# A four-layer attention and expert kernel on one core: the orders of its stages rewritten in four tables

## What is computed

```python
# L0
x = x + gate_a * (attend(q, k, v of modulate(ln(x)), 16 heads) @ W_proj)        # 256 keys
x = x + attend(ln(x) @ W_qc, ln(ctx) @ W_kvc) @ W_cproj                          # 1601 keys
x = x + gate_m * (gelu(modulate(ln(x)) @ W_mlp1) @ W_mlp2)
# L1
nx = layer_norm(x); w = softmax((nx @ Wq) @ (ctx @ Wk).T * H ** -0.5)            # one head, 1601 keys
combined = concat([nx, w @ (ctx @ Wv), anchor])
router = softmax(combined @ router_W + router_b)                                 # 3 experts
h = silu(combined @ e_w1 + e_b1); routed = sum(router * (h @ e_w2 + e_b2))
g = sigmoid(silu(combined @ gate_w1 + gate_b1) @ gate_w2 + gate_b2)
x = x + g * (routed @ out_w + out_b)
# L2
x = x + attend(ada_ln(x, t) @ Wq, ada_ln(ctx, t) @ Wkv) @ Wp                     # 1601 keys, 16 heads
# L3
x = x + g_sa * (attend(qkv of modulate(ln(x))) @ sa_proj_w)                      # 256 keys
x = x + attend(ln(x) @ q_w, ctx @ kv_w) @ ca_proj_w                              # 1601 keys
x = x + g_ff * (gelu(modulate(ln(x)) @ fc1_w) @ fc2_w)
```

## Time and profile before

| | before |
|---|---|
| median of 3 executions | 5056.57 us (5051.58 to 5058.7) |
| the profiled execution | 5052.83 us, of which the span of the profile is 5051.0 us |
| TensorE busy | 4586.7 us, 91% of the span, 47748 matmuls |
| DVE, ACT, POOL busy | 4001.8 us (79%), 3560.8 us (70%), 1628.4 us (32%) |
| granted clock of TensorE, mean of the span | 0.975 |
| DMA | 284.41 MB, mean 56 GB/s |

### The profile page before, as it was taken

How to read it: one execution, slowest core, us unless ns; L and a number is a source line. 1 busy time by engine, 2 the same in 40 slices (tenths; PEclk the granted TensorE clock), 3 DMA queues, 4 the chain that set the end, 5 groups by cost and what they waited for, 6 DMA issues and landing times.

```text
span 5051.0 us, 122456 instructions
## 1 busy us (share of the span) xinstructions
PE 4586.7 (91%) x47748; PEld 2149.7 (43%) x47748; DVE 4001.8 (79%) x8750; ACT 3560.8 (70%) x4867; POOL 1628.4 (32%) x2319
## 2 busy tenths in 40 slices
PE   5799999999998788868999999999999999999997
PEld 2344444444443577753333343443434443333333
DVE  5799899899886444427888888888998888888885
ACT  2387788787877344434777878878787777777776
POOL 4344444444431011032333242433223232323321
PEclk9799999999999899987999999999999999999998
DMA  2212212212111111111212122221221212112110
GB/s 68 70 54 60 65 52 70 62 48 71 50 47 37 62 55 54 61 51 48 62 49 71 55 65 60 56 75 46 71 58 55 67 44 62 56 47 67 38 56 8
DMA packets 347979, 284.41 MB, mean 56 GB/s; under 512 B 52775, under 2 KB 303866, under 8 KB 347404
## 3 DMA queue, kind: packets, MB, share of 16 engines
q1 hardware_dynamic: 339048, 273.29, 18.8%
q10 hardware_dynamic: 8356, 3.29, 0.3%
HBM read 86.98 MB, written 26.11 MB: 22 GB/s over the span
## 4 chain that ended last, share of the span: by engine, by line
PE 42%; ACT 5%; DVE 4%; issue 4%; ACTq 1%; POOL 0%; DMA 0%; SPq 0%; POOLq 0%; DVEq 0%
PE pb_obank L1158 15%; PE pb_dbank L1171 9%; PE pb_aunit L1134 7%; ACT pb_probs L949 4%; DVE pb_c_maxs L846 4%; PE pb_aunit L1208 2%; PE pb_aunit L1218 2%; PE pb_dbank L1233 1%; PE pb_aunit L1259 1%; PE pb_aunit L1253 1%; PE pb_aunit L1243 1%; PE pb_aunit L1188 1%; PE pb_aunit L1142 1%; PE pb_aunit L1197 1%; ACTq L942 1%
## 5 line engine op out<-in xcount | busy, mean ns | idle before, releaser
L846 DVE TENSOR_REDUCE pb_c_maxs<-pb_dbank 128x1 f32<-128x512 f32 (+1 forms) x3584 | 2046.0, 626 | 352.0 <-PE pb_dbank L1171 334.3
L949 ACT ACTIVATE pb_probs<-pb_aunit 128x1024 f32<-128x1024 f32 (+1 forms) x1792 | 1750.4, 1025 | 267.2 <-PE pb_aunit L1134 213.6
L846 DVE TENSOR_REDUCE pa_c_maxs<-pa_dbank 128x1 f32<-128x512 f32 (+1 forms) x1792 | 1024.4, 626 | 142.1 <-PE pa_dbank L1171 130.5
L949 ACT ACTIVATE pa_probs<-pa_aunit 128x1024 f32<-128x1024 f32 (+1 forms) x960 | 937.8, 1024 | 177.5 <-PE pa_aunit L1134 154.7
L1158 PE MATMUL pb_obank<-pb_probs,kept_vaug 128*9 128x256 f32 x13312 | 948.9, 382 | 2.1 <-ACT pb_probs L949 0.7
L1171 PE MATMUL pb_dbank<-kept_kst,kept_qst 62*128 62x512 bf16 (+1 forms) x4096 | 751.5, 341 | 41.4 <-DVE pb_c_maxs L846 32.3
L1134 PE MATMUL pb_aunit<-kept_qst,kept_kst 64*128 64x256 bf16 x6144 | 575.2, 273 | 102.7 <-ACT pb_probs L949 68.7
L1158 PE MATMUL pa_obank<-pa_probs,kept_vaug 128*9 128x256 f32 x6656 | 467.8, 381 | 1.3 <-ACT pa_probs L949 0.8
L1171 PEld LDWEIGHTS pb_dbank<-kept_kst,kept_qst 62*128 62x128 bf16 x4096 | 230.5, 93 | 559.3 <-DVE pb_c_maxs L846 397.0
L1171 PE MATMUL pa_dbank<-kept_kst,kept_qst 62*128 62x512 bf16 (+1 forms) x2048 | 390.2, 342 | 18.4 <-DVE pa_c_maxs L846 12.1
L1134 PEld LDWEIGHTS pb_aunit<-kept_qst,kept_kst 64*128 64x128 bf16 x6144 | 233.1, 95 | 401.2 <-ACT pb_probs L949 168.2
(11 more groups left out here) (526 smaller groups left out, 6134.4 us busy)
## 6 DMA issues: line engine op xcount, KB each, us to landing
kept_kst<-kept_keys SPq DMA_DIRECT2D x576, 200.1 KB
kept_cin<-in_ctx SPq DMA_DIRECT2D x37, 768.0 KB
context_turned<-moe_ct SPq DMA_DIRECT2D x16, 800.5 KB, 3.6
kept_qst<-pb_c_qsp SPq DMA_DIRECT2D x360, 32.0 KB
kept_turned<-context_turned SPq DMA_DIRECT2D x16, 400.5 KB
kept_turned<-context_turned SPq DMA_DIRECT2D x16, 400.0 KB
pa_z_kst<-pa_z_ksp SPq DMA_DIRECT2D x192, 32.0 KB
pb_z_qst<-pb_z_qsp SPq DMA_DIRECT2D x192, 32.0 KB
```

The lines of the kernel that those rows point to most:

```text
L846: dve.tensor_reduce(dst, dbank[N % RING_D][:, 0:cnt * width].rearrange("p (s c) -> p s c", s=cnt), AX.X, ALU.max).then_inc(d_free, 1)
L949: act.activation(probs[u % RING_P][0:rows].rearrange("p a i q -> p (a i q)"), src[0:rows, :], ACT.Exp, scale=HD ** -0.5).then_inc(a_free, 1)
```

## The change

The instructions stay the same. New are the order of the tokens in `expert_stages`, and in both tables the places of nearly all tokens, the shift of the maxima (`lead`) and two or three numbers of `rule`.

```diff
--- before.py
+++ after.py
@@ -294,24 +294,24 @@
 
 
 PLACES_LAYER0 = {
-    "c": {"st1": 0.0, "ldt": 0.0, "o0": 0.0546, "cs": 0.0597, "o1": 0.0629, "kq": 0.0637, "ot": 0.0975, "proj": 0.1314,
-          "v0": 0.1521, "ln2": 0.1524, "ca": 0.2037, "v1": 0.2734, "x2t": 0.2758, "h": 0.3617, "ctx0": 0.4189, "tanh": 0.456,
-          "k0": 0.4581, "ldx": 0.5108, "ctx1": 0.5254, "ldc": 0.5355, "ln": 0.6095, "gm": 0.6794, "fc2": 0.8253, "xt": 0.8404,
-          "k1": 0.888, "lda": 0.9058, "q": 0.9608, "ldr": 0.9684, "st2": 0.9847, "Rt": (0.0335, 0.0366)},
-    "z": {"o0": 0.1399, "o1": 0.2, "kq": 0.2689, "ln": 0.3441, "ot": 0.4104, "ldx": 0.4331, "proj": 0.4529, "st1": 0.4679,
-          "v0": 0.6946, "xt": 0.7521, "k0": 0.8115, "q": 0.9836, "lda": 0.9843, "ldr": 0.995, "Rt": (0.8668, 0.1855)},
-    "lead": 0.6118,
-    "rule": (0.189, 0.25, 2, 10),
+    "c": {"cs": 0.0061, "o0": 0.0526, "o1": 0.0531, "kq": 0.0887, "ot": 0.0975, "proj": 0.1305, "v0": 0.1376, "ln2": 0.1409,
+          "ca": 0.209, "v1": 0.2693, "x2t": 0.2758, "h": 0.3282, "ctx0": 0.4163, "tanh": 0.4548, "ldt": 0.4716, "k0": 0.4834,
+          "st1": 0.4903, "ctx1": 0.5368, "ldx": 0.5591, "ldc": 0.6081, "ln": 0.6098, "gm": 0.6271, "ldr": 0.7822,
+          "fc2": 0.8171, "xt": 0.8471, "st2": 0.8702, "k1": 0.8928, "q": 0.9551, "lda": 0.995, "Rt": (0.0326, 0.0366)},
+    "z": {"o0": 0.1041, "o1": 0.2673, "kq": 0.2717, "ln": 0.3546, "ot": 0.416, "proj": 0.4529, "st1": 0.482, "v0": 0.6946,
+          "xt": 0.7536, "k0": 0.9829, "ldx": 0.995, "q": 0.995, "lda": 0.995, "ldr": 0.995, "Rt": (1.3791, 0.1855)},
+    "lead": 0.6038,
+    "rule": (0.131, 0.199, 2, 8),
 }
 PLACES_LAYERS23 = {
-    "c": {"kq": 0.0, "v0": 0.0053, "cs": 0.0112, "ln": 0.0135, "o0": 0.0515, "o1": 0.0537, "ot": 0.0689, "ca": 0.1162,
-          "proj": 0.1281, "ldt": 0.161, "xt": 0.1932, "ldx": 0.2002, "v1": 0.2338, "ln2": 0.2863, "q": 0.3165, "x2t": 0.3622,
-          "h": 0.3645, "st1": 0.3835, "tanh": 0.4628, "ctx0": 0.4678, "ctx1": 0.4911, "gm": 0.519, "fc2": 0.7027,
-          "ldc": 0.7112, "st2": 0.7917, "k0": 0.8271, "k1": 0.889, "lda": 0.9368, "ldr": 0.9718, "Rt": (0.037, 0.0342)},
-    "z": {"ln": 0.0, "kq": 0.0, "o0": 0.2025, "v0": 0.2474, "o1": 0.2683, "xt": 0.2858, "lda": 0.3271, "ldx": 0.5735,
-          "k0": 0.6623, "ldr": 0.7338, "ot": 0.7813, "proj": 0.8126, "q": 0.9658, "st1": 0.9751, "Rt": (1.0687, 0.3224)},
-    "lead": 0.6065,
-    "rule": (0.202, 0.26, 2, 23),
+    "c": {"kq": 0.0, "cs": 0.0, "v0": 0.0074, "ln": 0.034, "o0": 0.051, "o1": 0.0546, "ot": 0.0674, "proj": 0.1281,
+          "ca": 0.1368, "xt": 0.226, "v1": 0.2295, "q": 0.2562, "ln2": 0.2834, "x2t": 0.3561, "ctx0": 0.3579, "h": 0.364,
+          "tanh": 0.4764, "ldt": 0.5, "gm": 0.5136, "st1": 0.514, "lda": 0.5308, "ctx1": 0.5764, "fc2": 0.6429, "ldr": 0.8137,
+          "k0": 0.8261, "k1": 0.889, "st2": 0.9889, "ldx": 0.995, "ldc": 0.995, "Rt": (0.0398, 0.0383)},
+    "z": {"kq": 0.0, "ln": 0.0051, "lda": 0.036, "o0": 0.0718, "v0": 0.2372, "o1": 0.2707, "xt": 0.3762, "ldr": 0.7463,
+          "k0": 0.7522, "ot": 0.786, "proj": 0.8119, "ldx": 0.8469, "q": 0.9583, "st1": 0.995, "Rt": (0.6344, 0.2557)},
+    "lead": 0.6086,
+    "rule": (0.202, 0.259, 2, 25),
 }
 
 
@@ -1429,10 +1429,10 @@
 
 def expert_stages(nb, groups):
 
-    plan = [("xt", 2), ("p", 1, 0, 0), ("h", 0, 0), ("qk", 2), ("x", 1, 1), ("p", 1, 0, 1), ("dn", 1), ("r", 0), ("h", 0, 1),
-            ("c", 2, 0), ("p", 1, 0, 2), ("p", 1, 0, 3), ("rb", 1), ("h", 0, 2), ("c", 2, 1), ("p", 1, 1, 0), ("c", 2, 2),
-            ("g1", 0), ("p", 1, 1, 1), ("c", 2, 3), ("s", 2, 0), ("p", 1, 1, 2), ("p", 1, 1, 3), ("e", 0, 0), ("e", 0, 1), ("g2", 0),
-            ("x", 2, 0), ("ln", 3), ("pc", 1), ("s", 2, 1), ("rt", 0), ("ev", 1), ("o", 0)]
+    plan = [("p", 1, 0, 2), ("p", 1, 0, 3), ("h", 0, 1), ("c", 2, 0), ("c", 2, 1), ("h", 0, 2), ("p", 1, 1, 0), ("rb", 1),
+            ("p", 1, 1, 1), ("g1", 0), ("c", 2, 2), ("p", 1, 1, 2), ("c", 2, 3), ("e", 0, 0), ("p", 1, 1, 3), ("e", 0, 1),
+            ("x", 2, 0), ("s", 2, 0), ("g2", 0), ("ln", 3), ("pc", 1), ("s", 2, 1), ("rt", 0), ("xt", 3), ("p", 2, 0, 0),
+            ("ev", 1), ("p", 2, 0, 1), ("qk", 3), ("x", 2, 1), ("o", 0), ("r", 1), ("dn", 2), ("h", 1, 0)]
     out = []
     for b in range(-3, nb):
         for tok in plan:
```

## The result

The changed kernel takes 4935.05 us, median of four executions (4930.74 to 4940.32); the kernel before took 5054.32 in four of the same comparison. The ratio is **0.9764**, 95% interval 0.9752 to 0.9776: 119 us less. The profiled execution took 4939.03 us with a span of 4937.2.

A forecast was written before the change was run, and what follows sets the result against it. TensorE, busy 91%, was taken as the bound, so only its idle 464 us could be won. The terms 67 + 3 + 8 + 5 + 5 = 88 us less gave 4966 us, with 4918 to 5018 as the range for 8 in 10.

The forecast's parts named there:

- 67 and 3: Expert layer: 67 us from fourteen bodies at 4.8 us saved each, plus 3 us from fewer clock falls.
- 28.7 + 0.3 = 29.0: Expert body's new pitch in us: TensorE's own 28.7 without waits, plus 0.3 for g1 and c2 coming late.
- The five causes: Expert body: late evacuations behind TensorE's waits at p(0,3), rb, h2, p(1,1) and s, 4.28 us printed, 5.1 with overlap.
- I take half back: Expert layer: of some 5 us lost to clock falls, 3 us come back, between 0 and 5.
- The first and last bodies stay: Expert layer: its first and last bodies are chains of single results and win nothing.
- Second phase, "8" and "5": Second attention phase: 8 us from ctx0 and q moved in the second layer, 5 us from q and fc2 in the last.
- q's term: Second attention phase: moving q ends a 0.39 us wait per body, in the second layer and in the last.
- First phase, "5": First attention layer: 0.3 us a body won of 2.9 idle, x 16 = 5 us, between -1 and +1 a body.
- At worst one q-like wait: Attention: SP's moved loads hold up the turned maxima's loads; zero cost, at worst 0.4 us x 30 = 12.
- Rival A: Expert layer: x0's exponentials ahead of g2t on ACT make xt late, 34 us given back, 5000 us; chance 0.15.
- Rival B: Attention bodies win half their idle time, 102 us in place of 18: 4882 us; a third gives 4916; chance 0.13.
- Rival C: Attention: DVE's maxima become the bound in pieces, 5103 us; slower once a body loses over 80 / 48 = 1.7 us; chance 0.07.

The follow-up runs named there:

- both small moves: The kernel before with s(0) moved behind e(0) and e(1) and r ahead of dn in the expert order: 5009.66 us, ratio 0.9913.
- the single moves: The kernel before with one expert-order move each: s(0) behind e(0) and e(1), 5051.63 us; r ahead of dn, 5040.0 us.
- the table alone: The kernel before with only the new places of the first attention phase (PLACES_LAYER0): 5044.52 us, ratio 0.9978.

## Why the prediction came out as it did

The sign and the place were right, and so was the mechanism in the expert layer, which has 87 of the 114 us. The time lies in the range for 8 in 10, but 5 us under the forecast's own range of 4940 to 4995; the forecast of 88 us less was 31 short. Errors did not cancel to bring it there: both large terms came out short, and the first phase's 5 us is small beside them.
- *Expert layer, "67 and 3"*: the stage won 87. The step "28.7 + 0.3 = 29.0" was mis-sized. The five causes went, and no small wait came in their place: 28.15. The floor of 28.7 was itself too high, by 0.55, because a wait costs more than the 0.16 of overlap beside its print. Read from start to start, against like groups without a wait, the five cost some 5.5 us for 4.28 printed: the products right behind a wait are slower too (h2's first pair 0.54 us for 0.43, the eight of s 2.77 for 2.70). And ev to o takes 0.72 us before (1947.23 to 1947.95), 0.43 from ev to the next group now (1906.15 to 1906.58), with no bracket in either. 14 x 0.85 is 12 us of the 17 that are missing.
- *The clock, "I take half back"*: all of it came back, 2 us more of the 17. That the last idle went is not what it took: with both small moves it came back with four waits left. As a mechanism it was underrated. The prediction took the falls as a small extra; the single moves show that they can take the whole gain of a change (34.2 where the waits alone give some 32.8).
- *"The first and last bodies stay"*: wrong by some 4 us. Of the 87.2, thirteen pitches have 77.3 (444.1 for 366.8, and 2074.6 - 1707.8, the first of its 28 xt products); 9.9 lie outside them. One body of these is in the prediction's fourteen, 33.80 - 28.15 = 5.65; the rest is what the ends won. (The changed kernel's thirteen pitches are 0.9 over 13 x 28.15, which is why 12, 2 and 4 make one more than 17.)
- *Second phase, "8" and "5"*: 27.5. The wait for `kept_turned` gave 0.5 of its 0.76 a body. q's term holds for L3 and has the wrong sign by itself for L2. Half of the gain or more came from places that the prediction had costed at nothing.
- *First phase, "5"*: -0.9 in the profile, 10.6 in the table alone. "At worst one q-like wait", 0.4 a body, named SP's queue rightly, and over eleven bodies of the profile it was 0.5 on average. But what TensorE waits for is the stacked q and k, and what puts them later is the new place of the turned maxima; in the prediction it was the loads `ldr` that held up the turned maxima.
- *Rival A* fell: its slack is 2.3, and putting x(0) back leaves the stage as it is. *Rival B* came in part: the attention phases won 26.6 us for the 18 forecast and its own 102. *Rival C* hardly came: on the page TensorE waits 39.6 us for DVE's maxima in the second phase (L1171) where it waited 32.3, 0.2 a body more. Its turning point is 70 / 48 = 1.5 us a body by its own gain of 70, not 80 / 48.
- *"What would show it"*: the steady pitches are 28.15 us for 28.3 to 30, 88.3 for 88.7, 78.7 for 79.5, and in the first phase 92.7 to 93.5 with one of 95.2, for 92.7. p(0,3), s and xt don't wait, and the second phase's scores don't wait for `kept_turned`.

## What to carry to other kernels

Where no engine is full, look for the evacuation that stands behind an unrelated operation in its engine's order; moving that operation was worth the printed waits and about a third more here (5.65 us for 4.28). Don't judge such moves one at a time: here one of them alone won nothing and two won 44 us, because the clock took the first one's gain; read the granted clock of each variant before dropping it. And a body that has become shorter meets the queue that was just in time before.

## What was not expected of the hardware

- The clock fell right behind waits of at most 1.3 us each: after 2.5 us with TensorE busy 1.12, or 3.5 us with 1.59, it was granted at 0.52 and 0.66 in the next 3 and 5 us. A fall cost 1.2 us in the kernel before and 1.7 with r ahead of dn, and bodies with the same waits had it or not. Taking one of five waits away made the falls more frequent, thirteen in thirteen pitches for four.
- SP took 38.75 us for 48 stacking DMAs in one execution and 37.85 in another of the same code of that phase. The 0.9 decides there whether TensorE waits.
